# Image loads moved ahead of the stack transfers on the sync queue, image transposes moved ahead of the first energy on TensorE

## The reference

```python
x = x + _L0_conv_ref(_gn(x), w_qkv, w_proj, b_proj)     # 8 heads of 32, within each row of 32 tokens
x = x + _L1_conv_ref(_gn(x), Wq, Wk, Wv, gamma)         # one head of 32, over all 1024 tokens
```

## Time and profile before

| what | value |
| --- | --- |
| time, median of 3 runs | 706.46 us (705.17 to 707.19) |
| the profiled execution's own time | 707.0 us |
| its span, first to last instruction | 705.2 us |
| busy share of the span: PE, DVE, ACT, POOL | 85%, 67%, 50%, 28% |
| mean granted clock of PE | 0.937 of full speed |
| moved by DMA | 47.53 MB, mean 67 GB/s |
| share of the chain that ended last: PE, DVE, ACT, DMA | 57%, 16%, 7%, 7% |

### The profile page before, as it was taken

The page is one execution under the profiler, slowest core; times in us unless marked ns, Lnnn a source line. Parts: engine busy times, 40 slices in busy tenths (PEclk is TensorE's granted clock), DMA queues, the critical chain, the costliest instruction groups (busy, mean ns, idle before and its releaser), DMA issues.

```text
span 705.2 us, 15145 instructions
## 1 busy us (share of the span) xinstructions
PE 600.5 (85%) x5859; PEld 435.3 (62%) x5859; DVE 472.2 (67%) x765; ACT 349.9 (50%) x486; POOL 197.1 (28%) x194
## 2 busy tenths in 40 slices
PE   2575595689899998999899989999899999649987
PEld 2254274347687676757576768767675767336756
DVE  4444247678866877687668886697668795774463
ACT  2532423286427852685338642884258622751363
POOL 5503132132126023513233213502342331201203
PEclk9796897599999999999999999999999999879999
DMA  4042222213232314241232223121324104201101
GB/s 156 0 121 61 56 64 83 61 45 73 70 85 69 75 32 114 76 106 32 82 89 82 67 80 75 64 71 34 105 80 105 32 24 106 75 0 38 47 1 60
DMA packets 40308, 47.53 MB, mean 67 GB/s; under 512 B 6848, under 2 KB 32320, under 8 KB 40256
## 3 DMA queue, kind: packets, MB, share of 16 engines
q1 hardware_dynamic: 36960, 43.47, 23.6%
q10 hardware_dynamic: 3296, 3.34, 1.4%
HBM read 10.09 MB, written 8.39 MB: 26 GB/s over the span
## 4 chain that ended last, share of the span: by engine, by line
PE 57%; DVE 16%; ACT 7%; DMA 7%; issue 6%; SPq 5%; POOL 1%; DVEq 0%; POOLq 0%; ACTq 0%
PE pb L253 8%; PE pb L254 7%; PE pb L255 7%; PE pa L253 6%; PE pa L254 6%; PE pa L255 6%; PE pb L557 4%; PE pa L491 4%; DMA xin<-in_x 4%; DVE max_neg L925 3%; PE pb L539 3%; DVE ast L827 2%; PE pa L393 2%; ACT e L749 2%; PE pa L464 2%
## 5 line engine op out<-in xcount | busy, mean ns | idle before, releaser
L925 DVE TENSOR_REDUCE max_neg<-pb 128x1 f32<-128x1024 f32 x64 | 78.0, 1218 | 76.9 <-PE pb L539 76.6
L253 PE MATMUL pb<-v_h,e_h 128*128 128x257 f16 x464 | 128.5, 277 | 0.0
L255 PE MATMUL pb<-v_h,e_l 128*128 128x257 f16 x464 | 127.4, 274 | 0.0
L254 PE MATMUL pb<-v_l,e_h 128*128 128x257 f16 x464 | 127.2, 274 | 0.0
L940 DVE TENSOR_TENSOR e_l<-e,e_h 128x1024 f16<-128x1024 f32 x64 | 77.8, 1223 | 17.6 <-ACT e L749 16.0
L1097 POOL TENSOR_TENSOR y<-qk_h,y 128x256 f32<-128x256 f32 x64 | 46.3, 726 | 137.0 <-ACT qk_h L758 136.9
L749 ACT ACTIVATE e<-pb,f_energy 128x1024 f32<-128x1024 f32 x64 | 71.3, 1113 | 16.2 <-PE pb L557 16.2
L758 ACT ACTIVATE qk_h<-pb,y_fac 128x256 f32<-128x256 f32 x58 | 27.4, 472 | 103.9 <-DVE y_fac L947 103.5
L1078 POOL TENSOR_TENSOR xb<-xin,bias 128x2048 f32<-128x2048 f32 x8 | 36.7, 4587 | 127.7 <-DVE x L905 127.7
L1083 POOL TENSOR_TENSOR before_turn<-before_turn,a_rinv 128x1024 f32<-128x1024 f32 x16 | 30.5, 1910 | 122.3 <-DVE a_rinv L886 122.3
L253 PE MATMUL pa<-a_nh,wqkv_h 128*128 128x512 f16 x128 | 49.8, 389 | 13.2 <-DVE before_turn L896 7.3
(11 more groups left out here) (136 smaller groups left out, 1378.4 us busy)
## 6 DMA issues: line engine op xcount, KB each, us to landing
xin<-in_x SPq DMA_DIRECT2D x16, 512.0 KB, 4.4
diag<-qkT SPq DMA_DIRECT2D x64, 128.0 KB, 2.3
diag<-turned SPq DMA_DIRECT2D x64, 128.0 KB, 2.4
turned<-before_turn SPq DMA_DIRECT2D x128, 64.0 KB, 2.0
out<-y SPq DMA_DIRECT2D x24, 256.0 KB, 2.1
out<-y ACTq DMA_DIRECT2D x8, 256.0 KB, 2.1
q_stack<-qk_hl SPq DMA_DIRECT2D x8, 128.0 KB, 2.3
k_stack<-qk_hl SPq DMA_DIRECT2D x8, 128.0 KB, 2.4
```

What stands on the lines that cost most here:

```text
L253: nc.tensor.matmul(out_ap, lh, rh, start=start, stop=False)
L254: nc.tensor.matmul(out_ap, lh, rl, start=False, stop=False)
L255: return nc.tensor.matmul(out_ap, ll, rh, start=False, stop=stop)
L925: nc.vector.tensor_reduce(max_neg[:, it:it + 1], pb[:, 0:2, :].rearrange("p a n -> p (a n)"), X, ALU.max, negate=True).then_inc(b_max, 1)
```

## The change

On the sync queue, the two loads of image i+3 go ahead of the four stack transfers of image i+1, for every step that has both (loads of images 2 to 7). On PE, the transposes of image i+2 go ahead of energy 0 of image i (steps 0 to 5; in steps -2 and -1 there is no energy). No wait is taken away or added.

```diff
@@ sync, second(i)
                 if f: k_spread(i + 2, 0)
                 if f: k_spread(i + 2, 1)
+                if more and m: load(i + 3)
                 if m: b_stacks(i + 1)
-                if more and m: load(i + 3)
@@ tensor, first(i), for it in range(4)
                     if o and not last_image(i - 1): b_output(i - 1, it, b, range(4, 8))
+                    if f and it == 1: transposes("a", i + 2, range(4))
                     if b and it >= 1: b_energy(i, (0, 2, 3)[it - 1], m)
-                    if f and it == 1: transposes("a", i + 2, range(4))
```

## The result

The changed kernel takes 689.66 us (median of 4 runs, 689.42 to 690.05) against 706.83 us of the kernel before (4 runs). The ratio is 0.9752, 95% interval 0.9715 to 0.9789. The profiled execution took 689.47 us, its span fell from 705.2 to 687.7 us (17.5), and the mean granted clock rose from 0.937 to 0.945 (by itself that says little: over the four runs of the changed kernel it lies between 0.945 and 0.960, and over the eleven runs of the kernel before beside e1 between 0.930 and 0.949).

A forecast was written before the change was run, and what follows sets the result against it. PE's wait for the image load was taken to lie on the path, DVE to limit after the first maximum. Steps 0 to 5 gain 1.5 + 2.78 + 1.78 + 3.75 + 3.30 + 3.95 = 17.1; 706.46 - 17.1 = 689.4 us, range 685 to 697.5.

The forecast's parts named there:

- Loads: Sync queue: loads issue behind the key spread, land before PE's transposes; stacks issue as before; cost zero, cover 12 us.
- Transposes, then energy 0 at free + 2.16: PE: transposes start once PE is free of output 1, take 2.16 us at full clock, then energy 0 begins.
- First to second maximum, 3.01: DVE: second row maximum starts 3.01 us behind the first, after two factor operations, a row sum and its reciprocal.
- Second maximum to group mean, 8.21: DVE: from second row maximum to the next image's group mean, 8.21 us without a gap.
- New stalls of PE on DVE: PE waits 0.1 us for the first maximum, 1.2 before energy 2, 0.3 before the group mean; 1.6 in all.
- The rest of the step moves with it, to the end: What the second maximum gains, the rest of the step gains; all 17.1 us reach the kernel's end.
- The half clock stays: Rival: PE's clock still falls in steps 1, 3, 4 and 5, losing 6.7 us of the gain: 696.0 us; chance 0.15.
- The third rival: Rival: the image isn't early, energy 0 stands behind waiting transposes, 0.4 us lost per step: 709.0 us; chance 0.04.

The follow-up runs named there:

- e1: Changed kernel with the transposes put back behind energy 0, so only the loads moved: 687.59 us, ratio 0.970 to the kernel before.
- e8: Changed kernel with the loads ahead of the four stack transfers but behind their wait for `qk_hl`: 706.26 us, ratio 0.9986 to the kernel before.
- e5: Changed kernel with one factor operation on DVE (L947) as `tensor_scalar` in place of `tensor_tensor`: 686.34 us, ratio 0.970 to the kernel before.
- e6: Changed kernel with DVE's second row sum ahead of the first maximum and the factor operation as `tensor_scalar`: 682.72 us, ratio 0.965.
- f3: The kernel of e6 (early row sum, `tensor_scalar`, transposes ahead) run again in another group: 681.21 us, ratio 0.9641 to the kernel before.
- e2: Changed kernel with the loads put back behind the stacks, so only the transposes moved: 719.97 us, ratio 1.0169 to the kernel before.
- e3: Changed kernel with DVE's second row sum of layer a moved ahead of the first row maximum: 688.04 us, ratio 0.9716 to the kernel before.
- e4: Changed kernel with DVE's second row sum ahead of the first maximum and the transposes behind energy 0: 688.83 us, ratio 0.9713.
- f1: Changed kernel with early row sum and `tensor_scalar`, but transposes behind energy 0: 687.43 us, ratio 0.9724 to the kernel before.
- e7: Changed kernel with the loads one place further ahead, between the two key spreads: 722.32 us, ratio 1.0208 to the kernel before.

## Why the prediction was right

The forecast was 689.4, the measured median 689.66; 17.1 us forecast, 17.5 in the spans and 17.2 in the medians. By its steps:

- **Loads.** Right. They issue behind the key spread and wait for nobody; the stacks keep their time; the key spread wasn't held up (L333 lands in 2.3 us in the median, at most 4.3, which were 2.3 and 4.2). e8 shows that the gain is the head start, e1 that it is the whole gain.
- **Transposes, then energy 0 at free + 2.16.** The sign right, the size not: they take 1.75 (334.43 to 336.18). The record of 2.32 in the earlier trace rows, read as work, held a hidden wait for the second half of the image: its ninth matmul begins at 271.38, some 0.4 us behind the eighth, where the others stand 0.1 apart.
- **First to second maximum, 3.01.** Measured 2.93 (336.81 to 339.74).
- **Second maximum to group mean, 8.21.** Measured 8.60 (339.74 to 348.34): the factor operation of output 2, 0.82 us in place of 0.16, stands still for POOL's probabilities, which the change moved against it. "From it to the group mean DVE has no gap" was right and not enough, since a busy operation can be a waiting one. This error of 0.39 and the one of 0.41 in the transposes cancel: by step, the sum is partly luck, though not in its cause.
- **New stalls of PE on DVE.** Forecast 0.1, 1.2 and 0.3; measured 0, 0.93 and 0.49 in step 3.
- **The rest of the step moves with it, to the end.** Nearly, and by luck. Step 0's second part gave 1.2 more (PE is free of output 1 of step 1 at 187.88 in place of 190.62, 2.74 earlier, where the group mean of step 0 was 1.52 earlier; so 4.15 in place of 2.78 in the table): the wait of `a_output` for its spread fell from 1.76 to 0.57 us, and its matmuls ran at full clock:

```profile
138.63 3.37 PE L491 MATMUL pa<-diag,v_tok 128*32 128x128 f32 x64 [1.76 <-DMA diag<-turned]
```

```profile
136.57 1.96 PE L491 MATMUL pa<-diag,v_tok 128*32 128x128 f32 x64 [0.57 <-DMA diag<-turned]
```

  The forecast had step 0 at half clock and nothing behind its group mean. This full clock isn't tied to the early load: the same matmuls take 1.95 to 1.96 us in both traces of the changed kernel, in e5, e6 and f3, and also in e2 and e8, but 3.20 to 3.64 in e1, e3, e4 and f1. What decides it stays open.

  Behind step 5 the shift was 19.07 at row maxima 597.36 and 578.29, and 17.75 at 644.42 and 626.67. 1.3 us went back there, in a part with half-clock stretches, which fall on other work than before; that they are the cause was only argued. So an unforeseen gain of 1.2 and an unforeseen loss of 1.3 cancel: without the loss, the shift would have been 19 and not 17.1.
- **The half clock stays** (rival). It didn't: 1.00 over steps 1 to 5. e8 also stands at 1.00 in steps 1 to 5, with two or three waits for transfers per step, none over 1.32 us (1.12, 1.14 and 0.34 in step 4), while e2 and e7, with one wait of over 3 us in each step, have 0.98 in each step from the group mean of step 1 to that of step 5. The swing by short idle times, for which the prediction named the Trainium skill (TensorE: Matmul & The Clock Gate, the same section), didn't show at waits of 0.93 and 0.49.
- **What the prediction didn't ask** is what each half is worth. Together they gave 17; the loads alone give as much by the traces (by the medians of two groups a little more), the transposes alone cost 12 (719.97 against 708.45). The mechanism named, DVE as the limit behind the first maximum, already implies it: with the image early, the move on PE only delays DVE's start. The third rival, the case of e2, was priced at 709.0, and e2 took 719.97.

## What to carry to other kernels

When a transfer is late, ask where in its queue it could already have been issued: here 12 us of idle queue stood ahead of a wait that had nothing to do with it, and one place further ahead was already a loss, because others then wait behind it. When two edits come together, work out each alone; one can be worthless until another engine's chain is shortened, and harmful without its partner. A busy record that is far longer than its twins, or a merged one, may hold a wait: compare it with its twins before it goes into a sum. An order that removes a wait on one engine is worth only what the next engine can use.

## What the runs showed of the hardware

- A DVE `tensor_tensor` on 128x1 elements with both inputs in SBUF took 0.16 us, but up to 1.92 us (e4) beside a POOL `tensor_tensor` that had begun first or at the same time, ending 0.01 to 0.02 us behind it in the rows shown (e3: 409.65 and 409.79 to begin, 411.56 and 411.57 to end). As `tensor_scalar` with the factor as scalar operand it took 0.212 to 0.215 us in all 64 cases of e5. The Trainium skill (SBUF — State Buffer, section "Who interferes with whom") says that a DVE instruction with two SBUF inputs contends with a POOL instruction that reads SBUF, that what they share is an exclusive lock, and that the order of issue decides who blocks; these rows agree.
- A transfer of 64 KB (the last of the stacks) issued right behind two of 512 KB landed in 4.2 us in the median in place of 2.0 (e8), one issued 12 us behind them in 2.0 (the changed kernel).
- PE's granted clock fell to half in each of steps 1 to 5 behind one wait of 3.29 us or more at the transposes (e2), and behind each of the five waits of 3.18 us or more at the scores between the group means of steps 0 and 5 (e7). With two waits one behind the other, 0.53 to 0.77 us and 2.10 to 2.39 us (the kernel before), it fell in four of the five steps: in step 1 behind 0.53 and 2.10, in step 2 not behind 0.60 and 2.11. In e8, where no wait for a transfer was over 1.32 us, it stood at full in all five. So the length of the waits alone doesn't decide it.
